# An LSTM recurrence: sigmoid of i and f first, sigmoid of o behind both halves, and f times c formed by itself

## The chip, the cores and the metric

The kernel runs on one core of a Trainium2 chip. The metric is the device time of one execution, in microseconds (us). The kernel before takes 2701.34 us, the median of three executions (2698.51 to 2701.63). A core has a matrix engine, TensorE (PE in the rows, its weight loads PEld), an elementwise engine, VectorE (DVE), an engine for functions such as sigmoid and tanh, ScalarE (ACT), a general engine, GpSimd (POOL), and SyncE (SP), which issues the DMA transfers here. Each engine works through its own list of instructions in order; between engines, and between dependent instructions of one engine, the program waits on semaphores.

## The reference

An LSTM of 512 steps over 32 sequences with 512 features and a state of 512, and a residual addition. Cut to what matters:

```python
xW = jnp.einsum('ntd,dg->ntg', x, Wx) + b          # x: 32 x 512 x 512, Wx: 512 x 2048
def step(carry, xw_t):
    prev_h, prev_c = carry
    a = xw_t + prev_h @ Wh                          # Wh: 512 x 2048
    i = jax.nn.sigmoid(a[:, :Hd])
    f = jax.nn.sigmoid(a[:, Hd:2 * Hd])
    o = jax.nn.sigmoid(a[:, 2 * Hd:3 * Hd])
    g = jnp.tanh(a[:, 3 * Hd:])
    next_c = f * prev_c + i * g
    next_h = o * jnp.tanh(next_c)
    return ((next_h, next_c), next_h)
# x + the h of every step
```

Every step needs the h of the step before, so the 512 steps are a chain.

## The kernel before

The 512 columns of the state are cut into 4 strips of 128 (j), and the 32 sequences of a strip stand in 32 of the 128 partitions. A tile of 128 x 128 so holds one gate for all sequences and the whole state. Z[s] is a PSUM bank of 128 x 512: the four gates i, f, o and g of one step side by side, 128 columns each. A matmul works on 32 columns of the array, and four of them, one for each strip, run beside each other: the rows show such groups as "128*32" with x4.

One step t has two kinds of matmuls. The recurrent part (`recurrent_part`) multiplies h of step t-1 with Wh and adds to Z[s]. h and Wh are held as sums of two 16-bit parts, and three of the four products are formed: 8 groups of four 512-wide matmuls for the high part of h (hT_hi with wh_hi and wh_lo), then 4 groups for the low part (hT_lo with wh_hi). The first four groups need only the first half of the columns of every strip (a = 0), the next four the second half (a = 1). The x part doesn't depend on h: products for steps to come, cut into 16-bit parts and combined so that a pair of steps costs fewer products. Behind each recurrent part stand 21 groups of four 256-wide matmuls of this kind (`third_products` and `first_product`, or `second_products` and `last_product`), into Z, run and extra. While PE works on them, the rest of the step goes round the other engines.

That round is, by engine, with a the half:

- ACT waits for `z_done` (the last recurrent matmul), then takes for a = 0 and then a = 1: sigmoid of i, f and o of the half in one instruction (L499, 128 x 192, from Z into act), and tanh of g (L501, 128 x 64, into gc). Then, when DVE has the new c, tanh of it (L505, into tanh_c), again for each half.
- DVE forms both products i g and f c of a half in one instruction (`products`, L745, 128 x 128: gc holds g and c side by side, act holds i and f side by side), adds them (`new_c`, L749), multiplies o, the scale and tanh c (`high_part_of_h`, L733, into h_hi), turns the half in 32 x 32 blocks (`turn_high_part`, L738, into hT_hi), and at the end forms the low part of h (L763, L765, L768) and the output (L775).
- PE starts the next recurrent part when the first half of hT_hi is there.

After each step's own instructions ACT and DVE have work on x for later steps: scalings, cuts, copies between banks (ACT L438 to L491), the sums and differences of forms, x_lo, transposes and scales (DVE L598 to L645). The order on each engine is written out by hand (`step` and `block` of each engine); there is no scheduler. DMAs are issued by SP alone, for x ahead of its use and for the output.

[...] A row names the waits in their order in the program: in `[waits tanh_g_done,sig_done]` the wait for tanh_g_done, which the source writes last, stands apart, and the instruction itself carries sig_done.

Of the kernel before, what the change touches and what calls it, by code (L numbers as in the profile page):

```python
# [10 lines left out]
ALU = mybir.AluOpType  # L11
ACT = mybir.ActivationFunctionType
# [3 lines left out]
def lstm_residual(nc, x, h0, Wx, Wh, bias, out):  # L16
# [14 lines left out]
    C = P  # L31
# [18 lines left out]
    with ctx:  # L50
        def sb(name, shape, dt=F32):
            return ctx.enter_context(nc.sbuf_tensor(name, shape, dt))

        def bank(name):
            return ctx.enter_context(nc.psum_tensor(name, [P, 512], F32))

        def sem(name):
            return ctx.enter_context(nc.semaphore(name))
# [27 lines left out]
        act = sb("act", [P, ZW])  # L86

        gc = sb("gc", [P, 2, 2, C // 2])
        igfc = sb("igfc", [P, 2, 2, C // 2])
# [30 lines left out]
        Z = [bank(f"Z{s}") for s in range(TB)]  # L120
# [65 lines left out]

        z_done = sem("z_done")
        sig_done = sem("sig_done")
        tanh_g_done = sem("tanh_g_done")
        igfc_done = sem("igfc_done")  # L190
        c_done = sem("c_done")
        tanh_c_done = sem("tanh_c_done")
# [19 lines left out]
        def half(tile, a):  # L212
            return tile[:, a * HC:(a + 1) * HC]

        def half_gates(tile, a):
            return tile.rearrange("p (g a c) -> p a g c", g=4, a=2)[:, a]
# [29 lines left out]
        def started(value):  # L246
            return not isinstance(value, int) or value > 0
# [183 lines left out]
        def _(sc):  # L431
# [61 lines left out]
            def step(t, n, s):  # L493
                if s == 0:
                    sc.wait_ge(z_unscale_set, n + 1)
                scale = 1.0 if isinstance(t, int) and t == 0 else z_unscale[:, :]
                sc.wait_ge(z_done, t + 1)
                for a in range(2):
                    nc.scalar.activation(half_gates(act, a)[:, 0:3], half_gates(Z[s], a)[:, 0:3],  # L499
                                         ACT.Sigmoid, scale=scale).then_inc(sig_done, 1)  # L500
                    nc.scalar.activation(gc[:, a, 0], half_gates(Z[s], a)[:, 3],  # L501
                                         ACT.Tanh, scale=scale).then_inc(tanh_g_done, 1)
                for a in range(2):
                    sc.wait_ge(c_done, 2 * t + 1 + a)
                    nc.scalar.activation(half(tanh_c, a), gc[:, a, 1], ACT.Tanh).then_inc(tanh_c_done, 1)  # L505
# [44 lines left out]
            def block(i, n, r):  # L550
                for s in range(TB):
                    step(n * TB + s, n, s)
                    if s == 0:
                        if within(2 * n + 1, NQ):
# [36 lines left out]
        def _(v):  # L591
# [137 lines left out]
                scale_block(2, 0)  # L729

            def high_part_of_h(t, a):
                v.wait_ge(tanh_c_done, 2 * t + 1 + a)
                nc.vector.scalar_tensor_tensor(half(h_hi, a), half_gates(act, a)[:, 2], h_scale[:, :], half(tanh_c, a),  # L733
                                               ALU.mult, ALU.mult).then_inc(h_hi_done, 1)

            def turn_high_part(t, a):
                v.wait_ge(h_hi_done, 2 * t + 1 + a)
                nc.vector.transpose(hT_hi[:, NCH // 2 * a:NCH // 2 * (a + 1), :],  # L738
                                    half(h_hi, a).rearrange("p (ch l) -> p ch l", l=L)).then_inc(hT_hi_done, 1)

            def products(t, a):

                v.wait_ge(sig_done, 2 * t + 1 + a)
                v.wait_ge(tanh_g_done, 2 * t + 1 + a)
                nc.vector.tensor_tensor(igfc[:, a], half_gates(act, a)[:, 0:2], gc[:, a], ALU.mult).then_inc(igfc_done, 1)  # L745

            def new_c(t, a):
                v.wait_ge(igfc_done, 2 * t + 1 + a)
                nc.vector.tensor_tensor(gc[:, a, 1], igfc[:, a, 1], igfc[:, a, 0], ALU.add).then_inc(c_done, 1)  # L749

            def step(t):
                products(t, 0)
                new_c(t, 0)
                products(t, 1)
                high_part_of_h(t, 0)
                new_c(t, 1)
                turn_high_part(t, 0)
                high_part_of_h(t, 1)
                turn_high_part(t, 1)
                if started(t):  # L760

                    v.wait_ge(y_done, t)
                nc.vector.tensor_tensor(h32[:, :], act[:, 2 * C:3 * C], tanh_c[:, :], ALU.mult).then_inc(h32_done, 1)  # L763
                v.wait_ge(h32_done, t + 1)
                nc.vector.scalar_tensor_tensor(h_lo[:, :], h32[:, :], h_scale[:, :], h_hi[:, :],  # L765
                                               ALU.mult, ALU.subtract).then_inc(h_lo_done, 1)
                v.wait_ge(h_lo_done, t + 1)
                nc.vector.transpose(hT_lo[:, :, :], h_lo[:, :].rearrange("p (ch l) -> p ch l", ch=NCH)).then_inc(hT_lo_done, 1)  # L768
# [8 lines left out]
            def block(i, n, r):  # L777
                for s in range(TB):
                    step(n * TB + s)
                    add_x(i, s, r)  # L780
                    if s == 0:
                        if within(2 * n + 1, NQ):
                            add_extra(2 * n + 1, 1)
                        if within(n + 2, NB):
                            first_forms(n + 2, r)
                    if s == 1:
                        if within(2 * n + 3, NQ):
                            cut_x_lo(2 * n + 3, 1 - r, 1)
                        if within(n + 3, NB):
                            turn_x(n + 3, 1 - r, i + 2 + r)  # L790
                    if s == 2:
                        if within(2 * n + 2, NQ):
                            add_extra(2 * n + 2, 0)
                        if within(n + 2, NB):
                            last_forms(n + 2, r)
                        if within(n + 1, NB):
                            set_h_scale(n + 1, 1 - r)
                    if s == 3:
                        if within(2 * n + 4, NQ):
                            cut_x_lo(2 * n + 4, r, 0)  # L800
                        if within(n + 3, NB):
                            scale_block(n + 3, 1 - r)
# [56 lines left out]
```

## Time and profile before

| | |
|---|---|
| device time, median of 3 | 2701.34 us (2698.51 to 2701.63) |
| the profiled execution | 2700.78 us, of which the span of instructions 2699.0 us |
| mean granted clock of TensorE | 0.988 of full |
| PE busy | 2611.6 us, 97% of the span |
| DVE busy | 2150.0 us, 80% |
| ACT busy | 1694.0 us, 63% |
| POOL busy | 72.4 us, 3% |

The span falls into a preparation of some 100 us (weights are loaded, scaled and cut) and 512 steps that look alike. PE's 97% is the union of matmuls that overlap each other in time: one 256-wide matmul is shown for 0.27 us, though the next group of four starts 0.11 us behind. A gap of a tenth of a microsecond in the stream of matmuls therefore hardly shows as idle time of PE. It shows in the starts of successive groups, and in the idle time of PEld.

### The profile page before, as it was taken

How to read it: one execution, taken by the hardware profiler on the slowest of the kernel's cores; microseconds unless marked ns; L12 is line 12 of the kernel's file. 1: busy time of each engine (PE TensorE's matmuls, PEld its weight loads, DVE VectorE, ACT ScalarE, POOL GpSimd, SP SyncE). 2: the span in 40 equal slices, each digit the busy share in tenths (PEclk: the TensorE clock that was granted, in tenths of full speed). 3: DMA queues.
4: the chain of work that ended last, by engine and by line, in shares of the span. 5: the costliest groups of instructions: out<-in, count | busy, mean ns of one | idle time of the engine just before them, and what ended most of it. 6: DMA issues, size and time to landing. Idle time of an engine off the chain costs nothing.

```text
span 2699.0 us, 163151 instructions
## 1 busy us (share of the span) xinstructions
PE 2611.6 (97%) x67528; PEld 1755.8 (65%) x67528; DVE 2150.0 (80%) x8259; ACT 1694.0 (63%) x5392; POOL 72.4 (3%) x138
## 2 busy tenths in 40 slices
PE   3599999999999999999999999999999999999998
PEld 0366666666666666666666666666666666666665
DVE  4888888888888888888888888888888888888876
ACT  2566666666666666666666666666666666666664
POOL 3000000000000000000000000000000000000000
PEclk7799999999999999999999999999999999999999
DMA  6011111111111111111111111111111111111111
GB/s 149 18 40 43 35 39 43 35 39 43 35 39 43 35 39 43 35 39 43 35 39 43 35 39 43 35 39 43 35 38 43 35 39 43 35 39 43 35 35 25
DMA packets 223517, 109.85 MB, mean 41 GB/s; under 512 B 25216, under 2 KB 222464, under 8 KB 222464
## 3 DMA queue, kind: packets, MB, share of 16 engines
q1 hardware_dynamic: 223488, 109.48, 16.2%
q8 instruction: 16, 0.26, 0.0%
q14 instruction: 13, 0.11, 0.0%
HBM read 75.83 MB, written 33.55 MB: 41 GB/s over the span
## 4 chain that ended last, share of the span: by engine, by line
PE 95%; DVE 1%; ACT 1%; issue 0%; DVEq 0%; ACTq 0%
PE Z L318 71%; PE run L318 18%; PE extra L318 6%; DVE wh_lo L681 0%; DVE gc L749 0%; ACT act L499 0%; DVE igfc L745 0%; DVE h_hi L733 0%; ACT tanh_c L505 0%; ACT wh_hi L524 0%; ACT gc L501 0%; DVE hT_hi L738 0%; DVE x_lo L615 0%; DVE zs L634 0%; DVE h_lo L765 0%
## 5 line engine op out<-in xcount | busy, mean ns | idle before, releaser
L318 PE MATMUL Z<-wh_hi,hT_hi 128*32 128x512 f16 x8176 | 801.5, 382 | 7.6 <-DVE hT_hi L738 6.4
L499 ACT ACTIVATE act<-Z,z_unscale 128x192 f32<-128x192 f32 x1022 | 431.1, 422 | 583.0 <-PE Z L318 583.0
L318 PE MATMUL Z<-wh_lo,hT_hi 128*32 128x512 f16 x8176 | 796.2, 379 | 0.0
L318 PE MATMUL Z<-wh_hi,hT_lo 128*32 128x512 f16 x8176 | 529.7, 379 | 0.0
L745 DVE TENSOR_TENSOR igfc<-act,gc 128x128 f32<-128x128 f32 x1024 | 299.6, 293 | 285.0 <-ACT gc L501 284.6
L318 PE MATMUL run<-wx_hi,x_hi 128*32 128x256 f16 x6120 | 433.1, 273 | 44.5 <-DVE x_lo L615 42.3
L505 ACT ACTIVATE tanh_c<-gc 128x64 f32<-128x64 f32 x1024 | 262.4, 256 | 339.3 <-DVE gc L749 339.3
L318 PEld LDWEIGHTS Z<-wh_hi,hT_hi 128*32 128x32 f16 x8176 | 214.6, 95 | 352.1 <-DVE hT_hi L738 234.8
L318 PE MATMUL run<-wx_lo,x_hi 128*32 128x256 f16 x6120 | 433.2, 273 | 0.0
L318 PE MATMUL run<-wx_hi,x_lo 128*32 128x256 f16 x6120 | 433.2, 273 | 0.0
L318 PE MATMUL Z<-wx_lo,x_hi 128*32 128x256 f16 x6120 | 432.8, 273 | 0.0
L318 PE MATMUL Z<-wx_hi,x_lo 128*32 128x256 f16 x6120 | 432.8, 273 | 0.0
L318 PE MATMUL Z<-wx_hi,x_hi 128*32 128x256 f16 x6120 | 432.8, 273 | 0.0
L733 DVE SCALAR_TENSOR_TENSOR h_hi<-act,h_scale,tanh_c 128x64 f16<-128x64 f32 x1024 | 291.8, 285 | 120.2 <-ACT tanh_c L505 85.9
L318 PEld LDWEIGHTS Z<-wh_hi,hT_lo 128*32 128x32 f16 x8176 | 215.4, 96 | 225.8 <-DVE hT_lo L768 113.5
L501 ACT ACTIVATE gc<-Z,z_unscale 128x64 f32<-128x64 f32 x1022 | 322.3, 315 | 0.0
L318 PEld LDWEIGHTS Z<-wh_lo,hT_hi 128*32 128x32 f16 x8176 | 218.4, 97 | 133.0 <-issue 0.7
L738 DVE STREAM_TRANSPOSE hT_hi<-h_hi 128x64 f16<-128x64 f16 x1024 | 247.6, 242 | 17.8
L749 DVE TENSOR_TENSOR gc<-igfc 128x64 f32<-128x64 f32 x1024 | 226.9, 222 | 17.4
L318 PEld LDWEIGHTS run<-wx_hi,x_hi 128*32 128x32 f16 x6120 | 164.1, 97 | 104.2 <-issue 41.6
L318 PEld LDWEIGHTS run<-wx_lo,x_hi 128*32 128x32 f16 x6120 | 164.1, 97 | 57.5
L765 DVE SCALAR_TENSOR_TENSOR h_lo<-h,h_scale,h_hi 128x128 f16<-128x128 f32 x512 | 180.3, 352 | 18.1
(88 smaller groups left out, 3586.6 us busy)
## 6 DMA issues: line engine op xcount, KB each, us to landing
x_in<-in_x SPq DMA_DIRECT2D x512, 64.0 KB, 2.1
x_res<-in_x SPq DMA_DIRECT2D x512, 64.0 KB, 2.1
out_y<-y SPq DMA_DIRECT2D x512, 64.0 KB, 1.7
wx_raw<-in_Wx SPq DMA_DIRECT2D x16, 256.0 KB, 9.1
wh_raw<-in_Wh SPq DMA_DIRECT2D x16, 256.0 KB, 20.0
bias_bc<-in_bias SPq DMA_DIRECT2D x4, 64.0 KB, 2.1
h_in<-in_h SPq DMA_DIRECT2D x4, 16.0 KB, 14.1
```

The costliest lines, as they stand in the source:

```text
L318: return nc.tensor.matmul(out, lhsT, rhs, start=False, stop=last, skip_group_check=True)
L499: nc.scalar.activation(half_gates(act, a)[:, 0:3], half_gates(Z[s], a)[:, 0:3], ACT.Sigmoid, scale=scale).then_inc(sig_done, 1)
L501: nc.scalar.activation(gc[:, a, 0], half_gates(Z[s], a)[:, 3], ACT.Tanh, scale=scale).then_inc(tanh_g_done, 1)
L505: nc.scalar.activation(half(tanh_c, a), gc[:, a, 1], ACT.Tanh).then_inc(tanh_c_done, 1)
L733: nc.vector.scalar_tensor_tensor(half(h_hi, a), half_gates(act, a)[:, 2], h_scale[:, :], half(tanh_c, a), ALU.mult, ALU.mult).then_inc(h_h ...
L738: nc.vector.transpose(hT_hi[:, NCH // 2 * a:NCH // 2 * (a + 1), :], half(h_hi, a).rearrange("p (ch l) -> p ch l", l=L)).then_inc(hT_hi_don ...
L745: nc.vector.tensor_tensor(igfc[:, a], half_gates(act, a)[:, 0:2], gc[:, a], ALU.mult).then_inc(igfc_done, 1)
L749: nc.vector.tensor_tensor(gc[:, a, 1], igfc[:, a, 1], igfc[:, a, 0], ALU.add).then_inc(c_done, 1)
L765: nc.vector.scalar_tensor_tensor(h_lo[:, :], h32[:, :], h_scale[:, :], h_hi[:, :], ALU.mult, ALU.subtract).then_inc(h_lo_done, 1)
```

## The change

Four edits, all inside one step of ACT and DVE.

- ACT: the sigmoid of a half takes the gates i and f alone (128 x 128 in place of 128 x 192). The sigmoid of o is one instruction for both halves (128 x 128), behind the tanh of g of the second half and ahead of the first tanh of c. It signals a semaphore of its own, sig_o_done.
- DVE, first half: f c is formed by its own instruction, 128 x 64, which waits for the sigmoid only, and i g by another, 128 x 64, which waits for tanh of g. The addition waits for both.
- DVE, second half: as before.
- DVE: the first `high_part_of_h` of a step waits for sig_o_done too.

```diff
                 for a in range(2):
-                    nc.scalar.activation(half_gates(act, a)[:, 0:3], half_gates(Z[s], a)[:, 0:3],
+                    nc.scalar.activation(half_gates(act, a)[:, 0:2], half_gates(Z[s], a)[:, 0:2],
                                          ACT.Sigmoid, scale=scale).then_inc(sig_done, 1)
                     nc.scalar.activation(gc[:, a, 0], half_gates(Z[s], a)[:, 3],
                                          ACT.Tanh, scale=scale).then_inc(tanh_g_done, 1)
+
+                nc.scalar.activation(act[:, 2 * C:3 * C], Z[s][:, 2 * C:3 * C],
+                                     ACT.Sigmoid, scale=scale).then_inc(sig_o_done, 1)
                 for a in range(2):
                     sc.wait_ge(c_done, 2 * t + 1 + a)
...
             def high_part_of_h(t, a):
+                if a == 0:
+                    v.wait_ge(sig_o_done, t + 1)
                 v.wait_ge(tanh_c_done, 2 * t + 1 + a)
...
+            def first_products(t):
+
+                v.wait_ge(sig_done, 2 * t + 1)
+                nc.vector.tensor_tensor(igfc[:, 0, 1], half_gates(act, 0)[:, 1], gc[:, 0, 1], ALU.mult).then_inc(fc_done, 1)
+                v.wait_ge(tanh_g_done, 2 * t + 1)
+                nc.vector.tensor_tensor(igfc[:, 0, 0], half_gates(act, 0)[:, 0], gc[:, 0, 0], ALU.mult).then_inc(ig_done, 1)
+
+            def first_c(t):
+                v.wait_ge(fc_done, t + 1)
+                v.wait_ge(ig_done, t + 1)
+                nc.vector.tensor_tensor(gc[:, 0, 1], igfc[:, 0, 1], igfc[:, 0, 0], ALU.add).then_inc(c_done, 1)
...
             def step(t):
-                products(t, 0)
-                new_c(t, 0)
-                products(t, 1)
+                first_products(t)
+                first_c(t)
+                last_products(t)
                 high_part_of_h(t, 0)
-                new_c(t, 1)
+                last_c(t)
```

`last_products` and `last_c` are `products` and `new_c` of before with a = 1.

On ACT one step of the loop read before (act, gc and tanh_c are written in SBUF, Z is the bank of the step):

```order
L499 ACTIVATE act<-Z,z_unscale 128x3x64 [waits z_done]
L501 ACTIVATE gc<-Z,z_unscale 128x64
L499 ACTIVATE act<-Z,z_unscale 128x3x64
L501 ACTIVATE gc<-Z,z_unscale 128x64
L504 ISA
L505 ACTIVATE tanh_c<-gc 128x64 [waits c_done]
L504 REGISTER_ALU
```

and reads now:

```order
L502 ACTIVATE act<-Z,z_unscale 128x2x64 [waits z_done]
L504 ACTIVATE gc<-Z,z_unscale 128x64
L502 ACTIVATE act<-Z,z_unscale 128x2x64
L504 ACTIVATE gc<-Z,z_unscale 128x64
L507 ACTIVATE act<-Z,z_unscale 128x128
L510 ISA
L511 ACTIVATE tanh_c<-gc 128x64 [waits c_done]
L510 REGISTER_ALU
```

One instruction has come in ahead of the first tanh of c, and the two in front of the tanhs of g are shorter; the line numbers have moved with the added code.

On DVE the head of a step, from the products to the first turned half, read before (the second REGISTER_ALU and the ISA row set registers that waits compare with):

```order
L743 ISA
L745 TENSOR_TENSOR igfc<-act,gc 128x128 [waits tanh_g_done,sig_done]
L749 TENSOR_TENSOR gc<-igfc 128x64 [waits igfc_done]
L743 REGISTER_ALU
L745 TENSOR_TENSOR igfc<-act,gc 128x128 [waits tanh_g_done,sig_done]
L733 SCALAR_TENSOR_TENSOR h_hi<-act,h_scale,tanh_c 128x64 [waits tanh_c_done]
L749 TENSOR_TENSOR gc<-igfc 128x64 [waits igfc_done]
L738 STREAM_TRANSPOSE hT_hi<-h_hi 128x64 [waits h_hi_done]
```

and reads now:

```order
L751 ISA
L752 TENSOR_TENSOR igfc<-act,gc 128x64 [waits sig_done]
L754 TENSOR_TENSOR igfc<-act,gc 128x64 [waits tanh_g_done]
L757 REGISTER_ALU
L759 TENSOR_TENSOR gc<-igfc 128x64 [waits ig_done,fc_done]
L763 REGISTER_ALU
L765 TENSOR_TENSOR igfc<-act,gc 128x128 [waits tanh_g_done,sig_done]
L741 SCALAR_TENSOR_TENSOR h_hi<-act,h_scale,tanh_c 128x64 [waits tanh_c_done,sig_o_done]
L769 TENSOR_TENSOR gc<-igfc 128x64 [waits igfc_done]
```

The first product of 128 x 128 has become two of 128 x 64, each with one wait. The first addition, which had one wait, now has ig_done apart and carries fc_done, and the first h_hi now has tanh_c_done apart and carries sig_o_done. The second product keeps its two waits.

## Rows read from the trace of the kernel before

**Rows 1.** The page: busy time of each engine, its share of the span, instructions.

```profile
PE 2611.6 (97%) x67528; PEld 1755.8 (65%) x67528; DVE 2150.0 (80%) x8259; ACT 1694.0 (63%) x5392; POOL 72.4 (3%) x138
```

**Rows 2.** Who waited for whom: us in total, times, longest.

```profile
ACT act L499 <- PE Z L318: 583.0, 511, 2.8
...
DVE igfc L745 <- ACT gc L501: 284.6, 511, 2.2
PEld Z L318 <- DVE hT_hi L738: 234.8, 1010, 2.8
PEld Z L318 <- DVE hT_lo L768: 113.5, 505, 0.2
```

**Rows 3.** Windows: length, busy us per engine (instructions), PEclk, DMA share, GB/s.

```profile
1500.00:2000.00 500.00, 499.95 (x13056) 338.60 (x13052) 404.71 (x1580) 322.05 (x1039) 8.46 (x24) 1.00 0.15 38
```

**Rows 4.** Timeline, PE: start, duration, instruction, xcount [idle before <-releaser].

```profile
1518.03 0.28 PE L318 MATMUL Z<-wx_lo,x_hi 128*32 128x256 f16 x4
1518.14 0.28 PE L318 MATMUL Z<-wx_hi,x_lo 128*32 128x256 f16 x4
1518.42 0.40 PE L318 MATMUL Z<-wh_hi,hT_hi 128*32 128x512 f16 x4
```

**Rows 5.** Timeline, PEld, same stretch: weight loads of the recurrent part.

```profile
1518.41 0.10 PEld L318 LDWEIGHTS Z<-wh_hi,hT_hi 128*32 128x32 f16 x4 [0.28 <-DVE hT_hi L738]
...
1519.15 0.10 PEld L318 LDWEIGHTS Z<-wh_hi,hT_hi 128*32 128x32 f16 x4 [0.18 <-DVE hT_hi L738]
```

**Rows 6.** Costliest groups of the page: busy us, mean ns | idle before.

```profile
L499 ACT ACTIVATE act<-Z,z_unscale 128x192 f32<-128x192 f32 x1022 | 431.1, 422 | 583.0 <-PE Z L318 583.0
```

**Rows 7.** Timeline, ACT, one step and the start of the next.

```profile
1516.18 0.42 ACT L499 ACTIVATE act<-Z,z_unscale 128x192 f32<-128x192 f32 x1 [1.29 <-PE Z L318]
1516.50 0.31 ACT L501 ACTIVATE gc<-Z,z_unscale 128x64 f32<-128x64 f32 x1
1516.70 0.42 ACT L499 ACTIVATE act<-Z,z_unscale 128x192 f32<-128x192 f32 x1
1517.00 0.32 ACT L501 ACTIVATE gc<-Z,z_unscale 128x64 f32<-128x64 f32 x1
1517.50 0.26 ACT L505 ACTIVATE tanh_c<-gc 128x64 f32<-128x64 f32 x1 [0.17 <-DVE gc L749]
1518.24 0.26 ACT L505 ACTIVATE tanh_c<-gc 128x64 f32<-128x64 f32 x1 [0.49 <-DVE gc L749]
...
1521.24 0.42 ACT L499 ACTIVATE act<-Z,z_unscale 128x192 f32<-128x192 f32 x1 [0.89 <-PE Z L318]
```

**Rows 8.** Timeline, DVE, the same step, the instructions ahead, and the next step's.

```profile
1515.70 0.28 DVE L608 TENSOR_TENSOR forms<-forms 128x128 f32<-128x128 f32 x1
1516.08 0.29 DVE L611 TENSOR_TENSOR forms<-forms 128x128 f32<-128x128 f32 x1
1516.29 0.15 DVE L645 COPY h_scale<-scales 128x1 f32<-128x1 f32 x1
1516.91 0.29 DVE L745 TENSOR_TENSOR igfc<-act,gc 128x128 f32<-128x128 f32 x1 [0.47 <-ACT gc L501]
1517.24 0.23 DVE L749 TENSOR_TENSOR gc<-igfc 128x64 f32<-128x64 f32 x1
1517.43 0.29 DVE L745 TENSOR_TENSOR igfc<-act,gc 128x128 f32<-128x128 f32 x1
1517.79 0.28 DVE L733 SCALAR_TENSOR_TENSOR h_hi<-act,h_scale,tanh_c 128x64 f16<-128x64 f32 x1
1517.99 0.22 DVE L749 TENSOR_TENSOR gc<-igfc 128x64 f32<-128x64 f32 x1
1518.12 0.24 DVE L738 STREAM_TRANSPOSE hT_hi<-h_hi 128x64 f16<-128x64 f16 x1
1518.53 0.28 DVE L733 SCALAR_TENSOR_TENSOR h_hi<-act,h_scale,tanh_c 128x64 f16<-128x64 f32 x1 [0.17 <-ACT tanh_c L505]
...
1521.38 0.22 DVE L640 SCALAR_TENSOR_TENSOR scales<-scale_mul,zs,scale_add 128x4 int32<-128x4 int32 x1
```

More of the change, by code:

```diff
@@ L188, in lstm_residual @@
         sig_done = sem("sig_done")
+        sig_o_done = sem("sig_o_done")
         tanh_g_done = sem("tanh_g_done")
+        fc_done = sem("fc_done")
+        ig_done = sem("ig_done")
         igfc_done = sem("igfc_done")
@@ L739, in turn_high_part, with last_products, last_c @@
                                     half(h_hi, a).rearrange("p (ch l) -> p ch l", l=L)).then_inc(hT_hi_done, 1)
[L741 to L749, printed above, removed]
+            def first_products(t):
[7 more added lines that the diff above has]
+                nc.vector.tensor_tensor(gc[:, 0, 1], igfc[:, 0, 1], igfc[:, 0, 0], ALU.add).then_inc(c_done, 1)
+            def last_products(t):
+                v.wait_ge(sig_done, 2 * t + 2)
+                v.wait_ge(tanh_g_done, 2 * t + 2)
+                nc.vector.tensor_tensor(igfc[:, 1], half_gates(act, 1)[:, 0:2], gc[:, 1], ALU.mult).then_inc(igfc_done, 1)
+            def last_c(t):
+                v.wait_ge(igfc_done, t + 1)
+                nc.vector.tensor_tensor(gc[:, 1, 1], igfc[:, 1, 1], igfc[:, 1, 0], ALU.add).then_inc(c_done, 1)
             def step(t):
-                products(t, 0)
-                new_c(t, 0)
-                products(t, 1)
+                first_products(t)
+                first_c(t)
+                last_products(t)
                 high_part_of_h(t, 0)
-                new_c(t, 1)
+                last_c(t)
                 turn_high_part(t, 0)
```

## The prediction

> **What bounds the kernel now.** I read the page first. PE is busy 97% of the span [rows 1], so the first question is whether PE is full or waits in gaps too short to show. [...] The list of waits comes next: PE's weight loads waited 234.8 us for hT_hi and 113.5 us for hT_lo [rows 2]. The timeline shows what these cost. Groups of the x part start 0.11 us apart (1518.03, 1518.14), and the first recurrent group starts 0.28 us behind the last of them (1518.42) [rows 4]. So PE's stream has a hole of 0.28 - 0.11 = 0.17 us in front of each recurrent part, ended by the first half of hT_hi: its weights were loaded at 1518.41 [rows 5], and the turned half was done at 1518.12 + 0.24 = 1518.36 [rows 8]. The second half makes its weight load wait 0.18 us [rows 5], but the recurrent groups last twice as long as x groups, and I take this load, and that for hT_lo, to be hidden behind groups that still stream.
>
> A step takes 1521.24 - 1516.18 = 5.06 us [rows 7], and two sigmoids stand in each, so that 1022 of them [rows 6] are 511 steps. The hole is worth at most 511 x 0.17 = 87 us. That caps the gain; a loss has no such cap. What decides is one chain, from the end of the recurrent part to the first half of hT_hi. In us from the first sigmoid's start (1516.18) it reads [rows 7, 8]: tanh of g starts at 0.32 and ends at 0.63; igfc 0.73; gc, the new c, 1.06 to 1.29; tanh_c 1.32 to 1.58; h_hi 1.61; hT_hi 1.94 to 2.18; PE about 2.24.
>
> **The change part by part.** Two prices are needed that the trace does not show directly.
>
> *ACT at 128 columns.* With 192 columns the next instruction starts 0.32 and 0.30 us later, with 64 columns 0.20 us later [rows 7]. Half-way in size is half-way in time: 0.25 to 0.26, I take 0.255, bounds 0.20 and 0.32 from the same rows. The duration, 0.42 at 192 and 0.31 at 64, becomes about 0.365.
>
> *A wait that stands apart.* Where an instruction carries the wait that ends last, it starts 0.03 to 0.04 us after the releaser's end: h_hi 0.03 after tanh_c (1517.76 to 1517.79, and 1518.50 to 1518.53), gc 0.04 after igfc (1517.20 to 1517.24). Where the deciding wait is the one apart, it starts 0.10 us after: igfc after tanh of g (1516.81 to 1516.91, and 1517.32 to 1517.43), and L611 of the same engine after L608 (1515.98 to 1516.08), whose separate wait is for L608 [rows 7, 8]. So I charge 0.07 us for each place where the separate wait decides, with bounds of 0 (if it is really something else in those three places) and 0.08.
>
> [...]
>
> Now the new chain, from the first sigmoid's start.
>
> - The sigmoid of i and f ends at 0.365. Tanh of g starts at 0.255 instead of 0.32 and ends at about 0.565.
> - f c starts 0.03 after the sigmoid, 0.395. It is of gc's kind and size, 0.22 long, and the next instruction can follow such a one after 0.13 (gc at 1517.99, hT_hi at 1518.12) [rows 8], so it is out of the way at 0.53. Nothing useful is queued behind it: what waits behind is i g, which can't go before 0.565.
> - i g now carries its only wait: 0.595 to 0.815. Before, igfc started at 0.73: 0.065 comes from the shorter sigmoid, 0.07 from the wait that no longer stands apart.
> - The addition waits for i g by a separate wait: 0.815 + 0.10 = 0.915, against 1.06. The 128-wide product had cost 0.33 to here, the 64-wide one costs 0.32: the smaller size is nearly eaten by the separate wait. It ends at 1.145.
> - Tanh of c could start at 1.175. ACT must have issued two sigmoids, two tanhs and the sigmoid of o: 0.255 + 0.20 + 0.255 + 0.20 + 0.255 = 1.165. It just fits, with 0.01 us to spare. So the sigmoid of o costs nothing here, hidden behind DVE's products and addition; without that cover it costs its whole 0.255. Behind it on ACT wait tanh_c, hence h_hi, hence PE.
> - Tanh of c ends at 1.175 + 0.26 = 1.435. The first h_hi waits for it by the separate wait, since it carries sig_o_done, which came long before (0.91 + 0.365 = 1.275): 1.435 + 0.10 = 1.535, against 1.61.
> - From there the order and the sizes are as before, so hT_hi and PE's start come 0.075 us earlier; with the two roundings I take 0.065, since the sums in hundredths leave 0.055 to 0.075.
>
> Second half: its tanh of g ends at 0.71 + 0.32 = 1.03, its product starts at 1.13 and can be followed 0.20 us later, well ahead of 1.535. The second addition stands behind h_hi as before (0.20 later), so the second half, hT_lo and PE's other two waits move along with the first, and none comes into view. DVE has the room for one instruction more: it sat idle 0.47 us before igfc in this step [rows 8]. f c needs DVE 0.34 us earlier than igfc did. The work ahead ends at 1516.29 + 0.15 = 1516.44, 0.26 after the sigmoid, and in the tightest step, with the scales, at 1521.38 + 0.22 = 1521.60, which is 0.36 after 1521.24, against the 0.395 that f c wants [rows 7, 8]. No DMA is issued in the moved steps; SP and POOL are passed by nothing. ACT's x work keeps its place behind the second tanh of c and moves with it.
>
> Sum: 511 x 0.065 = 33 us off 2700.78, the profiled execution (2699.0 of span and 1.8 around it), gives 2667.6. That execution lies 0.6 us below the median of 2701.34, so the forecast is 2668 us. The hole in PE's stream shrinks from 0.17 to about 0.10 us.
>
> **The rivals.**
>
> *The sigmoid of o holds up tanh of c, and the kernel gets slower.* ACT has five instructions ahead of tanh_c where it had four. If a 128-wide ACTIVATE takes s to the next, tanh_c starts at 3 s + 0.40 and h_hi at 3 s + 0.76; that passes the c path (s + 0.92) at s = 0.26 and the old h_hi (1.61) at s = 0.283. For it: 0.01 us of room is nothing, and the cost per instruction may not shrink with its size. Against it: 192 and 64 columns differ by 0.10 to 0.12 us. At the upper bound, s = 0.31, h_hi comes at 1.69, 0.08 late: 511 x 0.08 = 41 us, 2742. Between 0.26 and 0.283 part of the gain is left: 2668 to 2698.
>
> [...]
>
> *A separate wait costs nothing.* Then the 0.10 in the three places belongs to something else, say tanh of g being seen late. If it stays with tanh of g, i g starts at 0.665, the addition at 0.925, tanh_c at 1.185, h_hi at 1.475: 0.135 gained, 69 us, 2632. If it vanishes altogether, ACT's 1.165 decides, h_hi comes at 1.455: 79 us, 2622. Against both stands L611, an instruction that reads nothing of ACT.
>
> *PE does not follow.* The chain is shorter but something else holds the start of the recurrent part, or PE's hole opens at another place (the second half, hT_lo). For it: those weight loads do wait. Against it: they wait for instructions of the same chain, which all move. Time: 2701, no change.
>
> **How the numbers follow.** The forecast as worked out has 0.69; its own range, with s from 0.245 to 0.265 and the separate wait at 0.06 to 0.08, is 2655 to 2682. The free wait has 0.09 (2622 to 2645), the ACT queue with part of the gain left 0.08 (2682 to 2698), the ACT queue with a loss 0.09 (2700 to 2742), no change 0.05. About 0.2%, 5 us, is what a measurement of this kernel tells from nothing. Faster: 0.69 + 0.09 + most of 0.08 = 0.84; same: 0.05 and the rest of that, 0.07; slower 0.09. The range 2630 to 2690 leaves out the losses, no change, and the ends of the two cases beside the forecast, together just under 0.2.
>
> **What would show it.** Tanh of g 0.25 to 0.26 behind the sigmoid; i g 0.03 behind the end of tanh of g; the first addition and the first h_hi 0.10 behind what they wait for; tanh_c behind the addition by 0.03, with next to no idle time of ACT ahead of it; a step of 4.99 to 5.00 us; PEld's wait for hT_hi down from 234.8 us by some 30. If the first h_hi starts 0.03 behind tanh_c, the price of the separate wait was wrong; if tanh_c starts 0.05 or more behind the addition, it was the sigmoid of o.

## The result and the profile after

The changed kernel takes 2684.89 us, median of 4 (2683.53 to 2685.21), against 2700.64 for the kernel before. The ratio is 0.9942, with a 95% interval of 0.9925 to 0.9959: faster by 0.6%, 15.8 us. The forecast was 2668 with a range of 2630 to 2690. The time lies in the range; the gain of 15.8 us is a little under half of the 33 us that were forecast.

The page of the changed kernel, engines' busy time:

```profile
PE 2592.4 (97%) x67528; PEld 1757.0 (65%) x67528; DVE 2220.5 (83%) x8771; ACT 1725.9 (64%) x5904; POOL 72.8 (3%) x138
```

DVE and ACT each have one instruction a step more (8771 against 8259, 5904 against 5392 [rows 1]); their busy time alone does not tell what the change is worth. The waits of PE's weight loads:

```profile
PEld Z L321 <- DVE hT_hi L746: 219.0, 1009, 2.7
PEld Z L321 <- DVE hT_lo L788: 113.0, 504, 0.3
```

The wait for hT_hi fell from 234.8 to 219.0 us [rows 2], by 16, as much as the kernel gained. It was to fall by some 30. The next rows say where the other half is. First ACT, two steps and the start of a third (L502 is the sigmoid of i and f, L504 tanh of g, L507 the sigmoid of o, L511 tanh of c):

```profile
1506.78 0.37 ACT L502 ACTIVATE act<-Z,z_unscale 128x128 f32<-128x128 f32 x1 [1.29 <-PE Z L321]
1507.05 0.31 ACT L504 ACTIVATE gc<-Z,z_unscale 128x64 f32<-128x64 f32 x1
1507.24 0.37 ACT L502 ACTIVATE act<-Z,z_unscale 128x128 f32<-128x128 f32 x1
1507.49 0.32 ACT L504 ACTIVATE gc<-Z,z_unscale 128x64 f32<-128x64 f32 x1
1507.69 0.39 ACT L507 ACTIVATE act<-Z,z_unscale 128x128 f32<-128x128 f32 x1
1507.97 0.26 ACT L511 ACTIVATE tanh_c<-gc 128x64 f32<-128x64 f32 x1
...
1511.79 0.37 ACT L502 ACTIVATE act<-Z,z_unscale 128x128 f32<-128x128 f32 x1 [0.84 <-PE Z L321]
...
1513.18 0.26 ACT L511 ACTIVATE tanh_c<-gc 128x64 f32<-128x64 f32 x1
...
1516.99 0.37 ACT L502 ACTIVATE act<-Z,z_unscale 128x128 f32<-128x128 f32 x1 [1.29 <-PE Z L321]
```

The first step takes 1511.79 - 1506.78 = 5.01 us, where the kernel before had 5.06 [rows 7]. The second takes 1516.99 - 1511.79 = 5.20. In it tanh of c starts 1.39 behind the sigmoid, in the first 1.19. DVE shows why (L752 is f c, L754 i g, L759 the addition, L741 h_hi, L646 the scales):

```profile
1507.18 0.23 DVE L752 TENSOR_TENSOR igfc<-act,gc 128x64 f32<-128x64 f32 x1
1507.38 0.23 DVE L754 TENSOR_TENSOR igfc<-act,gc 128x64 f32<-128x64 f32 x1
1507.72 0.22 DVE L759 TENSOR_TENSOR gc<-igfc 128x64 f32<-128x64 f32 x1
...
1508.33 0.29 DVE L741 SCALAR_TENSOR_TENSOR h_hi<-act,h_scale,tanh_c 128x64 f16<-128x64 f32 x1
...
1511.92 0.22 DVE L646 SCALAR_TENSOR_TENSOR scales<-scale_mul,zs,scale_add 128x4 int32<-128x4 int32 x1
1512.45 0.22 DVE L752 TENSOR_TENSOR igfc<-act,gc 128x64 f32<-128x64 f32 x1 [0.31 <-ACT act L502]
...
1512.92 0.23 DVE L759 TENSOR_TENSOR gc<-igfc 128x64 f32<-128x64 f32 x1
...
1513.54 0.28 DVE L741 SCALAR_TENSOR_TENSOR h_hi<-act,h_scale,tanh_c 128x64 f16<-128x64 f32 x1
```

In the first step f c starts 0.40 behind the sigmoid, i g 0.60, 0.02 behind the end of tanh of g (1507.36), the addition 0.11 behind the end of i g, h_hi 0.10 behind the end of tanh_c (1508.23).

The waits that stand apart have rows of their own in the trace, which count as no busy time (EVENT_SEMAPHORE, under the line of the wait that the source writes last; duration in ns, first and last start). In the kernel before, each of the 1024 products of 128 x 128 and each of the 128 differences of L611 has one ahead of it:

```profile
L744 DVEq EVENT_SEMAPHORE  x1024: 21/21/50, 103.0 to 2692.6; - x171
L610 DVEq EVENT_SEMAPHORE  x128: 21/21/21, 88.0 to 2650.3; - x128
```

In the changed kernel the first h_hi of a step (L740), the addition of the first half (L758) and the second product (L764) have one each:

```profile
L740 DVEq EVENT_SEMAPHORE  x512: 21/21/21, 104.2 to 2677.4; - x171
L758 DVEq EVENT_SEMAPHORE  x512: 21/21/21, 103.6 to 2676.7; - x171
L764 DVEq EVENT_SEMAPHORE  x512: 21/21/21, 103.7 to 2676.9; - x171
```

The second addition (its wait is L768) and the turned halves (L745), which wait for one semaphore each, have none. In the first step above the row of L740 starts at 1508.266, 0.036 behind the end of tanh_c (1508.230), and h_hi 0.066 behind that row's start; the row of L758 starts 0.038 behind the end of i g (1507.612), and the addition 0.066 behind it. This holds for the instructions named and not for every place of the program: ahead of the first sigmoid of a block the source of the kernel before waits for two semaphores as well (z_unscale_set and z_done), and only 8 of the 128 blocks have such a row there (L497).

In the second step f c starts 0.66 behind the sigmoid. The scales ended at 1512.14, 0.35 behind it, and the sigmoid ended at 1512.16; DVE sat idle for another 0.29 us. (The list of waits puts this idle time down to ACT's sigmoid, the last semaphore that f c needed; but that had long been given.) Between the scales and this f c stands the branch of DVE's loop, the jump from the end of a pass back to its start: the loop has two blocks (eight steps) to a pass and 60 passes, so 59 jumps back. The trace has rows for it, though they count as no busy time. The jump (COMPARE_BRANCH) and the first register instruction behind it (x1, duration in ns, first and last start):

```profile
L261 DVEq COMPARE_BRANCH  x1: 56/56/56, 1512.0 to 1512.0; - x1
L261 DVEq FUSED_REGOPS  x1: 85/85/85, 1512.3 to 1512.3; - x1
```

To the nanosecond, the jump starts at 1512.003, 0.085 us after the start of the scales (not their end), and ends at 1512.059; the next row starts at 1512.322, 0.263 later, and f c 0.133 after that. Over the 59 jumps back the median from the end of the jump to the next row is 0.264 us.

By the starts of the sigmoids over the whole trace, 58 steps take 5.20 to 5.22 us, every eighth one, and nearly all others 5.005 to 5.01. In the first step of the other block of a pass, which has no branch in front, the same scales end at the same place, and f c starts at 0.40.

PE's stream in the first of the two steps:

```profile
1508.74 0.28 PE L321 MATMUL Z<-wx_hi,x_lo 128*32 128x256 f16 x4
1508.96 0.40 PE L321 MATMUL Z<-wh_hi,hT_hi 128*32 128x512 f16 x4
```

The hole is 0.22 - 0.11 = 0.11 us, where it was 0.17 [rows 4].

### The profile page after: what moved, and what is told of

It reads as the page before. It is cut to its first block, busy times and chain, and to the rows that moved or that the text cites. A ratio compares the mean times of both kernels' runs of the same rounds, so it can differ in the third digit from the quotient of the medians.

```text
span 2683.4 us, 164695 instructions
## 1 busy us (share of the span) xinstructions
PE 2592.4 (97%) x67528; PEld 1757.0 (65%) x67528; DVE 2220.5 (83%) x8771; ACT 1725.9 (64%) x5904; POOL 72.8 (3%) x138
## 4 chain that ended last, share of the span: by engine, by line
PE 79%; DVE 10%; ACT 4%; issue 3%; DVEq 1%; ACTq 0%
PE Z L321 60%; PE run L321 14%; PE extra L321 5%; DVE h_hi L741 2%; ACT tanh_c L511 2%; DVE x_lo L621 1%; ACT gc L504 1%; DVE hT_hi L746 1%; DVE h_lo L785 1%; ACT act L502 1%; DVE zs L640 1%; DVE gc L769 1%; ACT act L507 1%; DVE y L795 1%; DVE gc L759 1%
## 5 line engine op out<-in xcount | busy, mean ns | idle before, releaser
L502 ACT ACTIVATE act<-Z,z_unscale 128x128 f32<-128x128 f32 x1022 | 375.8, 368 | 569.9 <-PE Z L321 569.9
L511 ACT ACTIVATE tanh_c<-gc 128x64 f32<-128x64 f32 x1024 | 262.4, 256 | 291.9 <-DVE gc L769 284.4
L321 PEld LDWEIGHTS Z<-wh_hi,hT_hi 128*32 128x32 f16 x8176 | 214.6, 95 | 335.8 <-DVE hT_hi L746 219.0
L741 DVE SCALAR_TENSOR_TENSOR h_hi<-act,h_scale,tanh_c 128x64 f16<-128x64 f32 x1024 | 291.5, 285 | 149.7 <-ACT tanh_c L511 87.2
L321 PEld LDWEIGHTS Z<-wh_hi,hT_lo 128*32 128x32 f16 x8176 | 215.8, 96 | 226.2 <-DVE hT_lo L788 113.0
L504 ACT ACTIVATE gc<-Z,z_unscale 128x64 f32<-128x64 f32 x1022 | 321.7, 315 | 0.0
L752 DVE TENSOR_TENSOR igfc<-act,gc 128x64 f32<-128x64 f32 x512 | 115.5, 226 | 133.5 <-ACT act L502 112.7
L507 ACT ACTIVATE act<-Z,z_unscale 128x128 f32<-128x128 f32 x511 | 196.4, 384 | 0.0
```

The lines of the kernel that those rows point to most:

```text
L321: return nc.tensor.matmul(out, lhsT, rhs, start=False, stop=last, skip_group_check=True)
L502: nc.scalar.activation(half_gates(act, a)[:, 0:2], half_gates(Z[s], a)[:, 0:2], ACT.Sigmoid, scale=scale).then_inc(sig_done, 1)
L507: nc.scalar.activation(act[:, 2 * C:3 * C], Z[s][:, 2 * C:3 * C], ACT.Sigmoid, scale=scale).then_inc(sig_o_done, 1)
L752: nc.vector.tensor_tensor(igfc[:, 0, 1], half_gates(act, 0)[:, 1], gc[:, 0, 1], ALU.mult).then_inc(fc_done, 1)
```

## The experiments

Times are medians, each against the kernel before on the same chip. The theory going in was that two things had taken the missing part of the gain: 0.013 us a step in the chain itself, and 0.197 us in each of the some 60 steps behind DVE's loop branch (59, as counted above). The rival causes were the scale chain itself and the fetching of instructions.

### DVE's loop made long, in the changed kernel and in the one before

```diff
-            run_blocks(v, block)
+            def long_body(i):
+                for k in range(10):
+                    for r in range(BODY):
+                        block(i * 10 - 9 + k, (i * 10 - 9 + k) * BODY + r, r)
+            for r in range(BODY):
+                block(0, r, r)
+            with v.Fori(1, 7) as i:
+                long_body(i)
+            for i in range(61, NB // BODY):
+                for r in range(BODY):
+                    block(i, i * BODY + r, r)
```

Six passes of 20 blocks in place of 60 passes of two, on DVE alone.

> The changed kernel, with DVE's loop alone in 6 passes of ten block pairs in place of 60 passes of one; all other engines and every computation as they are. Theory A (DVE's loop branch): in the changed kernel the first step of a pass takes 5.205 us, the other steps 5.01 us, because f c comes 0.67 us behind the sigmoid there and not 0.40; the branch stands ahead of f c, and DVE's work before it ends at 0.35. With 54 passes fewer, 54 x 0.197 = 10.6 us less: 2674 us, and only six steps stay long. Rival B (what is late is the scale chain or the all-reduce of GpSimd that it waits for, which also stands at a block's end): these stay in every block, and the time stays at 2685. Rival C (fetching of instructions that are not at hand, whatever the loop): longer code makes it worse, above 2685.

Measured: 2704.84 us, ratio 1.0016 (1.0006 to 1.0026). Slower than the changed kernel by 20 us, and even than the one before.

> The kernel before, with the same long DVE loop. Theory A: DVE's first instruction of a step waited for tanh of g there until 0.73 us behind the sigmoid, and the branch is over at about 0.67, so it was hidden: no change, 2700.6 within 1 us. Rival: if the branch also cost time before the change, about 54 x 0.1 to 0.2 us would be gained, 2690 to 2695.

Measured: 2723.69 us, ratio 1.0091 (1.0074 to 1.0108): 23 us slower, where no change was expected.

Theory A failed as a forecast of the time, and rival C came true. DVE at the head of a long pass, the scales and f c:

```profile
953.12 0.22 DVE L646 SCALAR_TENSOR_TENSOR scales<-scale_mul,zs,scale_add 128x4 int32<-128x4 int32 x1
956.21 0.23 DVE L752 TENSOR_TENSOR igfc<-act,gc 128x64 f32<-128x64 f32 x1 [2.86 <-issue]
```

```profile
DVE igfc L752 <- issue: 15.3, 5, 3.3
```

```profile
L833 DVEq COMPARE_BRANCH  x1: 63/63/63, 953.2 to 953.2; - x1
L833 DVEq FUSED_REGOPS  x1: 98/98/98, 956.0 to 956.0; - x1
```

Here f c comes 2.87 us after the scales' end (953.34), with no engine to wait for ("issue"). The jump again starts 0.085 after the start of the scales, but the next row comes 2.71 us after its end, and 2.7 to 3.2 us in all five returns, where the short loop has 0.26. The whole step takes 9.44 us in place of 5.01. The five steps at the return of a long pass take 9.3 to 9.9 us, about 22 us too long together. Other steps at fixed places of the long pass take 0.1 to 0.35 us too long, 7 us in all. Against that, 108 of the 128 first steps of a block, with the scale chain in front of f c and most without a branch between them, take 5.005 to 5.01 us, where every second one took 5.20: rival B is out. The long loop in the kernel before shows the same idle time, where its short loop had 0.4 us of it:

```profile
DVE igfc L745 <- issue: 17.8, 11, 3.4
```

The page of each run has a row that bears on rival C: the packets of the DMA queue q14, which it names "instruction". The changed kernel has 15 of them in the whole span, and none between 200 and 2500 us of it. With the long loop there are 124, 106 of them in that stretch, 8 KB each, and the kernel before goes from 13 to 112 with its own. DVE's program is all that differs, so the added packets are its instructions. In that stretch of the long loop 43 steps are more than 0.03 us too long, and each of them has such a packet in it; at the return shown three start, at 952.73, 954.22 and 956.88. So the loss of the long loops goes with fetching, though 57 steps with a packet are not late, and each packet takes 0.3 to 1.1 us, so that the 2.7 us to the next row are not accounted for one by one.

The 0.26 us behind the short loop's jump are another matter. From 200 us on no instruction packet falls in that loop, and the same 0.264 us stand there in the kernel before and in the changed one. What the chip does in them no row tells.

### The two halves of the change, each by itself

ACT's part (sigmoid of o behind both halves, DVE's products whole):

```diff
-                    nc.scalar.activation(half_gates(act, a)[:, 0:3], half_gates(Z[s], a)[:, 0:3],
+                    nc.scalar.activation(half_gates(act, a)[:, 0:2], half_gates(Z[s], a)[:, 0:2],
...
+                nc.scalar.activation(act[:, 2 * C:3 * C], Z[s][:, 2 * C:3 * C],
+                                     ACT.Sigmoid, scale=scale).then_inc(sig_o_done, 1)
...
             def high_part_of_h(t, a):
+                if a == 0:
+                    v.wait_ge(sig_o_done, t + 1)
```

> The ACT part of the change alone, on the kernel before: sigmoid of i and f per half, sigmoid of o behind them, the first h_hi waits for it; DVE's products as before, 128 x 128. By the chain with a price of 0.07 us for a deciding wait that stands apart: tanh of g ends at 0.573, product 0.675, addition 1.00, tanh_c 1.26 to 1.52, h_hi 0.10 later at 1.62 against 1.604 before: 0.015 us a step worse, 2708 us. If the wait apart is free: h_hi at 1.55, 0.054 a step gained, 2673. The part alone would then be better than the whole change.

Measured: 2717.28 us, ratio 1.0064 (1.0047 to 1.0080). Slower, on the side of the theory, and 9 us more than it said. An ordinary step on DVE (L751 the product, L755 the addition, L739 h_hi; the sigmoid started at 1154.60):

```profile
1155.27 0.29 DVE L751 TENSOR_TENSOR igfc<-act,gc 128x128 f32<-128x128 f32 x1 [0.52 <-ACT gc L502]
1155.60 0.22 DVE L755 TENSOR_TENSOR gc<-igfc 128x64 f32<-128x64 f32 x1
...
1156.22 0.28 DVE L739 SCALAR_TENSOR_TENSOR h_hi<-act,h_scale,tanh_c 128x64 f16<-128x64 f32 x1 [0.15 <-ACT tanh_c L509]
```

The product starts at 0.67, the addition at 1.00, h_hi at 1.62, each as worked out. Such steps take 5.07 to 5.08 us, 0.015 more than before, 7 us in all. The other 9 us lie mostly in two steps of each pass. The step behind the branch takes 5.13, and in the third step of a pass, which has no branch, the product comes late for no reason that the trace names (sigmoid at 1134.22):

```profile
1133.67 0.71 DVE L602 STREAM_TRANSPOSE x_T<-x_in 128x512 f32<-128x512 f32 x1
1134.98 0.29 DVE L751 TENSOR_TENSOR igfc<-act,gc 128x128 f32<-128x128 f32 x1 [0.61 <-ACT gc L502]
```

That is 0.76 and not 0.67, in every pass, and such a step takes 5.165 us. Together about 60 x (0.055 + 0.09) = 8.7 us. The second place is not at the branch, and no instruction packet falls between 200 and 2500 us of this run either; what sets it stays open.

DVE's part (f c by itself, ACT as before, hence no wait for the sigmoid of o). It is the changed kernel with the ACT lines above and the wait for sig_o_done taken back:

> The DVE part alone, with ACT as before (sigmoid of i, f and o of a half in one instruction, so no wait for o): f c by itself, then i g. i g at 0.66 in place of the product at 0.73, addition at 0.99, tanh_c at 1.25, h_hi at 1.54 against 1.604: 0.066 a step, 33.7 us; the loop branch takes back 0.14 x 60 = 8.6 us. 2675.5 us, so better than the whole change by 9 us. If the ACT part is what brought the gain (shorter sigmoid ahead of tanh of g), this one stays near 2700.

Measured: 2675.40 us, ratio 0.9908 (0.9891 to 0.9924). As expected, and 9.5 us better than the whole change. ACT and DVE:

```profile
1112.02 0.42 ACT L501 ACTIVATE act<-Z,z_unscale 128x192 f32<-128x192 f32 x1 [1.30 <-PE Z L320]
...
1113.27 0.26 ACT L507 ACTIVATE tanh_c<-gc 128x64 f32<-128x64 f32 x1
```

```profile
1112.68 0.22 DVE L748 TENSOR_TENSOR igfc<-act,gc 128x64 f32<-128x64 f32 x1
1113.01 0.23 DVE L753 TENSOR_TENSOR gc<-igfc 128x64 f32<-128x64 f32 x1
...
1113.56 0.28 DVE L735 SCALAR_TENSOR_TENSOR h_hi<-act,h_scale,tanh_c 128x64 f16<-128x64 f32 x1
```

I g starts at 0.66, the addition at 0.99, tanh_c at 1.25, h_hi 0.03 behind its end, at 1.54. The whole change has h_hi at 1.55 (1506.78 to 1508.33): what the shorter sigmoid gives ahead of tanh of g (0.05), the wait apart ahead of h_hi takes back (0.07).

### The order of two waits

The changed kernel, with the wait that ends last carried by the first h_hi:

```diff
-                if a == 0:
-                    v.wait_ge(sig_o_done, t + 1)
                 v.wait_ge(tanh_c_done, 2 * t + 1 + a)
+                if a == 0:
+                    v.wait_ge(sig_o_done, t + 1)
```

> The changed kernel with the two waits of the first h_hi in the other order, so that the one for tanh of c, which ends last, is carried by the instruction and the one for the sigmoid of o stands apart. Theory (a deciding wait that stands apart costs 0.07 us): h_hi starts 0.033 behind the end of tanh_c and not 0.102, 511 x 0.069 = 35 us less than 2685: 2650 us. If a separate wait costs nothing: 2685, no change.

Measured: 2649.15 us, ratio 0.9813 (0.9797 to 0.9829), 36 us less than the changed kernel. Tanh_c on ACT and h_hi on DVE:

```profile
1103.32 0.26 ACT L511 ACTIVATE tanh_c<-gc 128x64 f32<-128x64 f32 x1
```

```profile
1103.61 0.29 DVE L741 SCALAR_TENSOR_TENSOR h_hi<-act,h_scale,tanh_c 128x64 f16<-128x64 f32 x1
```

0.03 from 1103.58 to 1103.61, where it was 0.10. The row of its own at L740 is that of sig_o_done now, and starts at 1103.461, 0.15 us ahead of h_hi:

```profile
L740 DVEq EVENT_SEMAPHORE  x1: 21/21/21, 1103.5 to 1103.5; - x1
```

Nothing else in the program differs from the changed kernel, so this is the price of the deciding wait that stands apart, 0.07 us a step.

The same in all three places (`first_c` waits for ig_done first, `last_products` for tanh_g_done first):

```diff
-                v.wait_ge(fc_done, t + 1)
                 v.wait_ge(ig_done, t + 1)
+                v.wait_ge(fc_done, t + 1)
...
-                v.wait_ge(sig_done, 2 * t + 2)
                 v.wait_ge(tanh_g_done, 2 * t + 2)
+                v.wait_ge(sig_done, 2 * t + 2)
```

> The changed kernel with the order of two waits turned round in all three places (first h_hi, first addition, second product), so that the later one is always carried. The addition comes at 0.866 in place of 0.936 and tanh_c could start at 1.12, but ACT has issued the sigmoid of o at 0.911 only, which keeps it busy for some 0.26: tanh_c at 1.17 in place of 1.194, h_hi at 1.46 in place of 1.553. 0.093 a step, 47 us, less 3 us in the loop's first steps: 2640 us. If ACT were not held by the sigmoid of o, h_hi would come at 1.41 and PE's hole would be closed, 2630 or less. If a wait apart is free: 2685.

Measured: 2638.09 us, ratio 0.9772 (0.9756 to 0.9789).

```profile
1095.71 0.37 ACT L502 ACTIVATE act<-Z,z_unscale 128x128 f32<-128x128 f32 x1 [1.30 <-PE Z L321]
...
1096.62 0.38 ACT L507 ACTIVATE act<-Z,z_unscale 128x128 f32<-128x128 f32 x1
1096.87 0.28 ACT L511 ACTIVATE tanh_c<-gc 128x64 f32<-128x64 f32 x1
```

```profile
1096.32 0.23 DVE L754 TENSOR_TENSOR igfc<-act,gc 128x64 f32<-128x64 f32 x1
1096.58 0.22 DVE L759 TENSOR_TENSOR gc<-igfc 128x64 f32<-128x64 f32 x1
...
1097.18 0.28 DVE L741 SCALAR_TENSOR_TENSOR h_hi<-act,h_scale,tanh_c 128x64 f16<-128x64 f32 x1
```

The addition starts 0.03 behind i g (1096.55) and ends at 1096.80, 1.09 behind the sigmoid. Tanh_c starts at 1096.87 only, 0.25 behind the sigmoid of o: ACT holds it. That is the rival of the prediction in small. It decides once the waits are out of the way, and costs 0.04 us here.

The kernel before, with nothing but this order changed in `products`:

```diff
-                v.wait_ge(sig_done, 2 * t + 1 + a)
                 v.wait_ge(tanh_g_done, 2 * t + 1 + a)
+                v.wait_ge(sig_done, 2 * t + 1 + a)
```

> The kernel before, with nothing changed but the order of the two waits ahead of each 128 x 128 product, so that the one for tanh of g is carried. The product starts at 0.66 behind the sigmoid in place of 0.73, and everything behind it moves along: 511 x 0.069 = 35 us, of which the loop's first steps give back up to 60 x 0.07 = 4: 2666 to 2670 us, a larger gain than the whole change. If a wait apart is free: 2700, no change.

Measured: 2667.21 us, ratio 0.9880 (0.9864 to 0.9897). Two lines exchanged are worth 33 us, twice the change.

```profile
1106.98 0.42 ACT L499 ACTIVATE act<-Z,z_unscale 128x192 f32<-128x192 f32 x1 [1.30 <-PE Z L318]
1107.30 0.31 ACT L501 ACTIVATE gc<-Z,z_unscale 128x64 f32<-128x64 f32 x1
```

```profile
1107.64 0.29 DVE L745 TENSOR_TENSOR igfc<-act,gc 128x128 f32<-128x128 f32 x1 [0.65 <-ACT gc L501]
...
1108.51 0.28 DVE L733 SCALAR_TENSOR_TENSOR h_hi<-act,h_scale,tanh_c 128x64 f16<-128x64 f32 x1
```

The product starts 0.03 behind tanh of g (1107.61), at 0.66, and h_hi at 1.53.

### The branch put where DVE has time

```diff
+            def turned_body(i):
+                block(i, i * BODY, 0, range(1, TB))
+                block(i, i * BODY + 1, 1)
+                block(i + 1, i * BODY + BODY, 0, range(1))
+            block(0, 0, 0, range(1))
+            turned_body(0)
+            with v.Fori(1, 61) as i:
+                turned_body(i)
```

`block` takes the steps that it makes; the rest of the 64 pairs follows unrolled.

> The changed kernel with DVE's loop turned by one step: the same 60 passes of the same length, but a pass begins at the second step of its first block, so that the branch stands behind the two sums of forms, which end 0.00 us behind the next sigmoid, and not behind the scale chain, which ends 0.35 behind it. Theory: the first DVE instruction behind a branch starts about 0.32 us after the end of what stands before it; here at 0.32, ahead of the 0.40 at which f c is wanted, so that the 60 long steps of 5.205 us go: 60 x 0.197 = 11.8 us less, 2673 us. If the delay has to do with the scale chain or the place in the block rather than with the branch, 2685. An instruction fetch at another place of the stream may add some hundredths to one step of a pass.

Measured: 2673.18 us, ratio 0.9902 (0.9885 to 0.9918), 11.7 us less than the changed kernel. The steps of 5.20 us are gone: of the 128 first steps of a block 127 take 5.005 to 5.01, and of the second steps, where the branch now stands, 125. DVE at the branch (the sigmoid started at 1108.86):

```profile
1108.58 0.28 DVE L610 TENSOR_TENSOR forms<-forms 128x128 f32<-128x128 f32 x1
1109.26 0.23 DVE L752 TENSOR_TENSOR igfc<-act,gc 128x64 f32<-128x64 f32 x1 [0.40 <-ACT act L502]
```

Forms end at 1108.86, f c starts 0.40 later, when the sigmoid allows it. The rows of the jump (L833 here) show that the delay went along with it: at this pass the jump starts at 1107.8 and the next row at 1108.1, and over the 59 jumps the median from the jump's end to that row is 0.264 us, as before the turn. It costs nothing here. In every pass the jump starts some 0.60 us ahead of the first of the two sums of forms that come before it in the program, so DVE still had work in hand while the jump was under way. At the old place the jump came only 0.085 us after the scales had started. The scales carry a wait for the instruction before them (zs), which fits a jump that has to stay behind that wait, but no run puts this to the test.

### All together

The DVE part, with the waits in order and the loop turned:

> The DVE part of the change alone (ACT as in the kernel before, one sigmoid for i, f and o of a half), with the later wait carried in the addition and in the second product, and DVE's loop turned by one step. i g at 0.66, addition at 0.92, tanh_c at 1.18, h_hi at 1.47 against 1.604: 0.136 a step, 69.5 us, and nothing lost at the branch: 2631 us. If f c by itself brings less once the waits are in order, it stays near the 2667 of the kernel before with its waits turned round.

Measured: 2631.70 us, ratio 0.9747 (0.9731 to 0.9763). ACT, DVE and PE:

```profile
1092.65 0.42 ACT L501 ACTIVATE act<-Z,z_unscale 128x192 f32<-128x192 f32 x1 [1.29 <-PE Z L320]
...
1093.83 0.26 ACT L507 ACTIVATE tanh_c<-gc 128x64 f32<-128x64 f32 x1
```

```profile
1094.12 0.28 DVE L735 SCALAR_TENSOR_TENSOR h_hi<-act,h_scale,tanh_c 128x64 f16<-128x64 f32 x1
```

```profile
1094.61 0.28 PE L320 MATMUL Z<-wx_hi,x_lo 128*32 128x256 f16 x4
1094.75 0.40 PE L320 MATMUL Z<-wh_hi,hT_hi 128*32 128x512 f16 x4
```

Tanh_c at 1.18, h_hi at 1.47, and PE's hole is down to 0.14 - 0.11 = 0.03 us.

> The whole change with the waits of all three places in order and DVE's loop turned by one step. Tanh_c is held by the sigmoid of o on ACT (1.157), h_hi at 1.468, a step of 4.925 us in all places of a pass: 9 us less than the 2638 of the unturned loop, 2629 us. So within 3 us of the kernel that has the DVE part alone: with the waits in order, the sigmoid of o moved behind brings next to nothing.

Measured: 2634.33 us, ratio 0.9754 (0.9738 to 0.9770). The intervals overlap; the move of the sigmoid of o brings nothing that can be told here. It was expected at 2629, and of the 9 us for the turned loop 4 came. The steps behind the branch are short again (4.925 to 4.93), so the missing 5 us are not there: 3.3 of them lie in two single steps of the profiled execution, the very first (8.0 us against 6.3 in the unturned kernel) and the last but one (6.55 against about 5). What lengthens those stays open. They vary between the runs without regard to the variant: the first step takes 7.6 us in the kernel before, 6.4 in the changed one and 8.9 with DVE's part alone.

## Why the prediction was right and wrong

*What bounds the kernel.* Right. The hole ahead of the recurrent part was the place, and each variant but the two long loops moved the time, to some 2 us, by 511 times what its first h_hi moved, less what was lost at the branch and, with ACT's part alone, in the third step. The second half and hT_lo did not come into view: PE's wait for hT_lo stayed at 113.0 us. The recurrent groups start 0.22 us apart (1518.42, 1518.64 and 1518.86 in the kernel before), where groups of the x part start 0.11 apart. The granted clock was 1.00 from 1500 to 2000 us in the changed kernel too, as before [rows 3].

*ACT at 128 columns.* Taken at 0.255 from start to start, measured 0.27, 0.25 and, for the sigmoid of o, 0.25 (1096.62 to 1096.87, in the run with all waits exchanged, where ACT holds tanh_c). The first was 0.01 too small, and all that follows came 0.01 late.

*A wait apart.* Right, 0.07 us, in both new places, now shown by exchanging two lines: h_hi went from 0.10 behind the end of tanh_c to 0.03, and the addition, by the medians over 512 steps, from 0.104 behind the end of i g to 0.034. The rival by which it is free is out.

*The chain's sum.* Forecast: h_hi 0.065 us earlier. Measured: 1.55 against 1.61, and PE's start, by the medians over all steps without a branch, 0.051 earlier. I g was 0.226 long, not 0.22, and tanh_c came at 1.194, not 1.175. A step took 5.009 us against 5.061: 511 x 0.052 = 26.6 us in place of 33. That is a term mis-sized by a fifth, through small errors that all went one way: tanh of g, the product, the addition's start, and h_hi of before, which by the median over its steps came at 1.604 and not 1.61.

*"DVE has the room for one instruction more."* This step failed. The prediction compared the end of the scales, 0.36 behind the sigmoid, with the 0.395 at which f c is wanted, and put at nothing what stands between the two in one block out of two: the branch of DVE's loop. Behind it f c starts 0.31 us after the end of the scales (1512.14 to 1512.45), at 0.66. Before the change DVE's first instruction of a step started at 0.73 [rows 8] and all but hid that; f c, wanted at 0.40, does not. 59 x 0.197 = 11.6 us, and 26.6 - 11.6 = 15.0 against 15.6 between the profiled executions (2700.78 and 2685.21); the last 0.6 are what these steps had lost before the change. The run with the turned loop takes 11.7 us less, and its ordinary steps are as long as before.

The row with which to see it was there, in the kernel before. The step that starts at 1521.24, whose scales the prediction called the tightest case, is one behind the branch:

```profile
1521.98 0.29 DVE L745 TENSOR_TENSOR igfc<-act,gc 128x128 f32<-128x128 f32 x1 [0.38 <-ACT gc L501]
```

Its product starts at 0.74. By the medians over the trace it is 0.736 behind the branch and 0.728 elsewhere, and such a step takes 5.071 us in place of 5.061: the branch already ended last there, by 0.01 us. With the order of its waits exchanged this kernel has the product at 0.736 there still, and at 0.656 elsewhere.

In these 59 steps the change even costs time, 5.206 us against 5.071. By the medians f c starts at 0.668 and i g ends at 1.029, just where the whole product had ended. So f c by itself brings nothing there, and the two waits apart, ahead of the addition (at 1.133, where it was 1.063) and ahead of h_hi, cost their 0.07 us each.

That the time fell into the range all the same is owed to the width of the range, 22 us above the forecast. Of the reasons that the prediction gives for its range, none is the branch.

*The sigmoid of o on ACT.* It did not hold tanh_c in the changed kernel (the addition did, 0.03 behind), as forecast, but only because the wait apart made the addition late. The rival's loss was also priced too low for its own bound: the rows gave 0.32 as the upper bound and the sum used 0.31; with 0.32 h_hi comes at 1.72, 0.11 late, and the loss is 56 us and not 41.

## What to carry to other kernels

Where an instruction waits for two semaphores, see to it that the one that ends last is the one that it carries, here the one that the source writes first; a wait apart cost 0.07 us here each time it decided. Where an instruction is moved earlier on an engine, look at everything between it and the instruction before, the loop's branch too: what hid the branch may be the very wait that was removed. Here the branch cost nothing behind two sums that the engine still had in hand, and 0.197 us a pass behind the last of a chain of instructions that wait for each other. And try the halves of a change apart. Here the half with f c alone is better than the whole.

## What the runs showed of the hardware

- On DVE, in a loop of eight steps, the first row behind the jump back starts 0.26 us after the jump's end (median 0.264 over 59 jumps, in the kernel before, the changed one and the one with the turned loop alike), with no instruction packet between 200 and 2500 us. In a loop of 80 steps it was 2.7 to 3.2 us (five jumps), and the step took 9.3 to 9.9 us in place of 5.01.
- The jump did not wait for the work in front of it: its row started 0.085 us after the start of the scales, and in the turned loop some 0.60 us ahead of the start of the two sums that precede it in the program.
- A tenfold unrolled loop made the kernel 23 us slower with the branch hidden, and 20 us slower with it exposed; the packets of the "instruction" queue went from 13 to 112 and from 15 to 124.
- In the run with ACT's part alone the third step of a pass, away from any branch, took 0.09 us more than its neighbours in each pass. The cause is not known.
- A wait in an instruction of its own cost 0.07 us where it ended last (h_hi 0.10 behind tanh_c in the changed kernel), and nothing that shows where it ended before (0.03 with the waits exchanged, as in the kernel before, where h_hi had one wait). Its row took 21 ns, and in the step read of the changed kernel the first h_hi and the first addition started 0.066 us behind the start of theirs.
